# The first keys, values and queries of the cross attention computed in the slot attention's last rounds

## The reference

```python
# slot attention (L0_attn), 16 heads of 128, 64 slots
q, k = rope(hs @ Wq.T), rope(hs @ Wk.T);  v = hs @ Wv.T;  g = hs @ Wg.T
s  = clip(hs @ Ws1.T @ Ws2.T + bs2, -32, 32)
es, enz = exp(s), exp(-cumlogsumexp(s))
A  = tril(q @ k.T * scale)
qv = softmax(enz * (A @ es))
W2 = tril((qv * enz) @ es.T);  o = W2 @ v
out = (rms(o) * g_norm * silu(g)) @ Wo.T
# cross attention (L0_xattn), 16 heads of 16, 257 image and 1344 text keys
q = rms_norm(x @ q_w.T + q_b, norm_q_w)
k, v         = rms_norm(txt @ k_w.T + k_b, norm_k_w),         txt @ v_w.T + v_b
k_img, v_img = rms_norm(img @ k_img_w.T + k_img_b, norm_k_img_w), img @ v_img_w.T + v_img_b
out = (attention(q, k_img, v_img) + attention(q, k, v)) @ o_w.T + o_b
```

## Time and profile before

| | |
|---|---|
| median of 3 runs | 2198.05 us (2189.47 to 2202.49) |
| profiled execution | 2200.9 us |
| its span, first to last instruction | 2199.2 us |
| mean granted TensorE clock | 0.908 |
| busy PE, DVE, ACT, POOL | 1807.4, 1362.2, 839.0, 467.6 us |
| slot attention, from the trace | 0 to 685.6 us |
| cross attention, first load to first exponential's scores | 685.66 to 828.85 us |

### The profile page before, as it was taken

One profiled execution on the slowest core, in us unless ns is written; L12 is line 12 of the kernel. 1 busy time (PEld: TensorE's weight loads), 2 busy tenths in 40 slices (PEclk: granted clock), 3 DMA queues, 4 the chain that ended last, 5 costly groups with the idle time before them and its releaser, 6 DMA issues.

```text
span 2199.2 us, 32217 instructions
## 1 busy us (share of the span) xinstructions
PE 1807.4 (82%) x12150; PEld 1121.8 (51%) x12150; DVE 1362.2 (62%) x3113; ACT 839.0 (38%) x1339; POOL 467.6 (21%) x694
## 2 busy tenths in 40 slices
PE   5789888888864738898998997998597598899977
PEld 4678778777753203343443444565254244444446
DVE  4665666666643645868777844343546587888844
ACT  2233333333321203554645561343122145566652
POOL 4243433433211200201001003143100011311110
PEclk8899999999986758999999997999798789899989
DMA  3010000000004391441726307263722116556100
GB/s 125 1 30 10 20 20 11 10 1 1 1 1 104 125 146 34 91 61 41 127 43 108 44 2 273 96 235 117 130 59 41 51 27 113 92 89 74 28 1 20
DMA packets 88996, 142.96 MB, mean 65 GB/s; under 512 B 14421, under 2 KB 56537, under 8 KB 88842
## 3 DMA queue, kind: packets, MB, share of 16 engines
q1 hardware_dynamic: 74658, 116.05, 25.8%
q10 hardware_dynamic: 12312, 19.71, 3.2%
q0 software_dynamic: 1872, 5.13, 0.6%
HBM read 108.28 MB, written 32.03 MB: 64 GB/s over the span
## 4 chain that ended last, share of the span: by engine, by line
PE 57%; DVE 19%; issue 7%; DMA 6%; ACT 6%; POOL 2%; SPq 2%; ACTq 1%; another core or an unknown queue 0%; POOLq 0%; DVEq 0%
PE bank L1101 8%; PE bank L1061 8%; PE bank L1080 6%; PE bank L1416 5%; PE bank L1751 5%; PE bank L651 3%; PE bank L1647 3%; PE bank L1770 2%; PE bank L1648 2%; PE bank L1649 2%; DVE xa_part_max L1174 2%; PE bank L2160 2%; DMA xa_qst<-xa_negT 1%; PE bank L2145 1%; PE bank L616 1%
## 5 line engine op out<-in xcount | busy, mean ns | idle before, releaser
L1174 DVE TENSOR_REDUCE xa_part_max<-bank 128x1 f32<-128x448 f32 (+1 forms) x512 | 273.7, 569 | 87.2 <-PE bank L1061 82.4
L1135 ACT ACTIVATE xa_e<-bank 128x1024 f32<-128x1024 f32 (+1 forms) x208 | 212.6, 1022 | 146.6 <-PE bank L1080 144.8
L1135 ACT ACTIVATE ca_e<-bank 128x1024 f32<-128x1024 f32 (+2 forms) x208 | 196.4, 956 | 99.7 <-PE bank L1080 90.8
L1174 DVE TENSOR_REDUCE ca_part_max<-bank 128x1 f32<-128x400 f32 (+1 forms) x384 | 205.8, 570 | 35.5 <-PE bank L1061 31.6
L1061 PE MATMUL bank<-xa_kst,xa_qst 122*128 122x448 bf16 (+1 forms) x512 | 172.8, 364 | 45.5 <-issue 25.3
L1061 PE MATMUL bank<-ca_kst,ca_qst 125*128 125x400 bf16 (+2 forms) x512 | 160.3, 349 | 24.9 <-DMA ca_qst<-ca_q_parts 11.9
L1080 PE MATMUL bank<-xa_qst,xa_kst 128*128 128x256 bf16 (+1 forms) x832 | 130.1, 280 | 23.7 <-DMA xa_qst<-xa_negT 23.7
L1101 PE MATMUL bank<-xa_e,xa_vaug 128*17 128x256 f32 (+2 forms) x1792 | 142.3, 393 | 1.6 <-ACT xa_e L1135 0.6
L853 POOL TENSOR_TENSOR gsa_qk<-gsa_qk,gsa_rot 128x512 f32<-128x512 f32 x64 | 81.8, 1278 | 260.6 <-DVE gsa_rot L771 260.6
L1101 PE MATMUL bank<-ca_e,ca_vaug 128*17 128x256 f32 (+2 forms) x1664 | 125.8, 375 | 9.3 <-ACT ca_e L1135 8.4
L1061 PEld LDWEIGHTS bank<-xa_kst,xa_qst 122*128 122x128 bf16 x512 | 48.7, 99 | 155.0 <-DVE xa_part_max L1174 80.4
(11 more groups left out here) (366 smaller groups left out, 4000.7 us busy)
## 6 DMA issues: line engine op xcount, KB each, us to landing
xa_kst<-xa_k_parts SPq DMA_DIRECT2D x96, 200.1 KB, 8.7
ca_kst<-ca_k_parts SPq DMA_DIRECT2D x96, 200.1 KB, 7.4
xa_k_parts<-xa_parts SPq DMA_DIRECT2D x8, 1200.8 KB, 6.5
ca_k_parts<-moe_ctx_parts SPq DMA_DIRECT2D x8, 1200.8 KB
moe_gu<-in_expert_gate_up SPq DMA_DIRECT2D x8, 1024.0 KB
shared<-in_ctxT_split ACTq DMA_DIRECT2D x4, 1601.0 KB, 6.8
moe_ctxT<-in_ctxT SPq DMA_DIRECT2D x8, 800.5 KB, 8.1
ca_cv<-in_ctx ACTq DMA_DIRECT2D x4, 1536.0 KB
```

Of the source, the lines that this page charges most:

```text
L1135: e.activation(self.e[m % 3][0:rows, :, first:T], banks[m % 2][0:rows].rearrange("p a (h t) -> p (a h) t", t=T)[:, :, first:T], ACT.Exp, s ...
L1174: e.tensor_reduce(top, work[:, 0:hi - lo], AX.X, ALU.max).then_inc(*reduced(t, *step))
```

## The change

1. Buffers. `shared` (the context) is allocated outside both stages, so it may be filled during the slot attention. The slot attention's raw weights share two buffers instead of four (q with v, k with g), `clip` is gone (clipping writes into `es`, and the wait for its readers moves from ScalarE to VectorE), and tensors are laid out so that what the cross attention needs first lies on buffers whose last reader is early. The queries get a buffer of their own, two tiles and three parts large.
2. Steps. `xa_early` adds: context fetch and weights in round 12, biases and clearing of `xa_vaug0` in round 14, keys and values of batch 0 (13 `kv` tiles) in round 16, queries of batch 0 and the turning of the keys in round 17, queries of batches 1 and 2 in round 18. The queries of batch 3 are spread over the first units of the cross attention. `behind` starts after 8 steps of a round instead of 4.
3. PSUM rings by the engine that empties them: banks 0 and 1 VectorE, bank 2 `ok` alone, 3 to 5 ScalarE, 6 and 7 both. All moved steps work on banks 0 and 1.
4. The stage of the cross attention starts with the loads of the stacks; weights for its output and the copies into `places_h` follow. The constant rows are bf16 in the table and go from DRAM straight into the stacks. In the differential attention they are loaded at the stage's start into a buffer of their own; VectorE casts nothing.

```diff
-        w_raw = {key: sb(f"w{key}", [P, DC, GK]) for key in LINEAR}
+        raws = [sb(f"w{i}", [P, DC, GK]) for i in range(2)]
+        w_raw = {key: raws[key in "kg"] for key in LINEAR}
...
+            def xa_early(m):
+
+                if m == GSA_UNITS - 4:
+                    yield "fetch", 0
+                    yield "xa_w", 0
+                if m == GSA_UNITS - 2:
+                    yield "xa_w", 1
+                    yield "xa_const", 0
+                if m == GSA_UNITS:
+                    yield "xa_w", 2
+                    for n in range(XA_TILES):
+                        yield "kv", 0, n
+                    yield "fetch", 1
+                if m == GSA_UNITS + 1:
+                    yield from queries(0)
+                    yield "k_norm", 0
+                    yield from xa_keys(0)
+                if m == GSA_UNITS + 2:
+                    yield from queries(1)
+                    yield from queries(2)
...
-                yield from weave(list(weave(list(scores(m)), list(ahead(m)))), list(behind(m)), lead=4)
+                main = list(weave(list(weave(list(scores(m)), list(ahead(m)))), list(behind(m)), lead=8))
+                yield from weave(main, list(xa_early(m)))
...
-        gsa_front, gsa_back = Ring(3), Ring(3)
+        on_dve, on_act, on_both, xa_r1 = Ring(2), Ring(3), Ring(2), Ring(2)
         gsa_order = placed(gsa_steps(), {
+            "es": [(on_dve, clipped)], "cs": [(on_dve, enz_ready)], "qk": [(on_dve, rotated)],
+            "u": [(on_act, u_ready)], "et": [(on_act, et_ready)], "v": [(on_act, v_ready)], "a": [(on_act, a_copied)],
+            "z": [(on_act, z_ready)], "w2": [(on_act, w2_copied)], "ot": [(on_act, ot_ready)],
+            "gate": [(on_both, g_ready)], "o": [(on_both, o_ready)], "wo": [(on_both, x_ready)],
+            "norm_turn": [(on_both, hT_ready)],
...
-                    if k == 0 and unit >= 2:
-                        q.wait_ge(ok_taken, unit - 2)
+                    if k == 0 and unit:
+                        q.wait_ge(ok_taken, unit - 1)
...
-            parts = [list(XA.flow()), [(-100, ("fetch", 0))], spread(queries(), -100, -80)]
-            for b in range(B):
+            parts = [list(XA.flow()), spread(queries(B - 1), 4, 10)]
+            for b in range(1, B):
...
         def xa_sp(q):
             e = q.e
+            for n in range(AHEAD):
+                XA.load_sp(q, n)
+            e.dma_start(xwo[:], a["xa_o_w"].rearrange("(c p) n -> p c n", p=P)).then_inc(*xo_in("xa", by=16))
+            e.dma_start(bo[:], a["xa_o_b"].partition_broadcast(P)).then_inc(*xo_in("xa", by=16))
             e.dma_start(wgate[:], a["gate_w"].rearrange("(c p) n -> p c n", p=P)).then_inc(*gate_in("moe", by=16))
             e.dma_start(h_dram[:, D:D + 2], a["unsent"]).then_inc(*places_filled("moe", by=16))
...
         def da_act(q):
             e = q.e
+            ca_stacks.constants_load(q, ca_aug[:])
...
-                elif kind == "ahead" and n == 0:
-                    ca_stacks.constants_dve(q, cv[:].rearrange("p n d -> p (n d)")[:, 0:CTX])
```

More of the change, by code:

```diff
@@ L94, in const_table @@
     put("sin", np.concatenate([np.sin(ang), -np.sin(ang)], 0).astype(np.float32))
[L96 to L100, removed]
+    aug = np.zeros((P, CTX + CTX % 2), np.uint16)
+    one = np.uint16(0x3F80)
+    aug[REST - 6:REST - 3, :TXT] = one
+    aug[REST - 3:REST, TXT:CTX] = one
+    aug[2 * REST - 3:2 * REST] = one
+    put("aug", aug.view(np.float32))
     key = np.arange(CTX)
@@ L194, in placed @@
 def placed(steps, rings, *tag):
-    return [(step, [ring.take(signal, *(() if step[0] == "norm_turn" else tag), *step) for ring, signal in rings.get(step[0], ())])
+    return [(step, [ring.take(signal, *(own or (() if step[0] == "norm_turn" else tag)), *step) for ring, signal, *own in rings.get(step[0], ())])
             for step in steps]
@@ L537, in gsa_pe @@
                 if kind == "norm_turn":
-                    norm_pe(q, step, places, bank[5:8])
+                    norm_pe(q, step, places, bank[6:8])
+                    continue
+                if kind in XA_EARLY:
+                    xa_pe_step(q, step, places, bank[0:2])
                     continue
@@ L541, in gsa_pe @@
                     (j, free), = places
-                    ps = bank[5 + j] if kind in ("z", "w2", "gate", "o", "ot", "wo") else bank[j]
+                    ps = home(kind, j)
                     if free:
@@ L694, in gsa_act @@
                     q.wait_ge(v_mm, n, i)
-                    e.copy(v[n % 2][:, i, :], bank[j]).then_inc(*v_ready(*step))
+                    e.copy(v[n % 2][:, i, :], home(kind, j)).then_inc(*v_ready(*step))
                 elif kind == "a":
@@ L705, in gsa_act @@
                 elif kind == "z":
-                    ps, zb = bank[5 + j], qz[n % 2]
+                    ps, zb = home(kind, j), qz[n % 2]
                     if n < 2:
@@ new lines, in __init__, with constants_load, constants_act @@
+                row = 0 if sets == 2 else REST
+                self.aug = a["consts"][row:row + REST, lo:hi].bitcast(BF16)[:, 0:keys]
+            def constants_load(self, q, to):
+                q.e.dma_start(to, self.aug).then_inc(*self.aug_in(self.tag, by=16))
+            def constants_act(self, q, staged=None):
+                aug = self.aug if staged is None else staged
+                if staged is not None:
+                    q.wait_ge(self.aug_in, self.tag)
+                for t in self.kst:
+                    q.e.dma_start(t[self.rows], aug.unsqueeze(1).broadcast_to([REST, UNIT, self.keys])).then_inc(*self.aug_copied(self.tag, by=16))
@@ L1385, in build, with xa_pe_step @@
             "out_turn": [(xa_work, out_copied)], "out": [(xa_work, x_ready)], "norm_turn": [(xa_work, hT_ready)]}, "xa")
+        def xa_pe_step(q, step, places, work):
+            e = q.e
+            kind, n, *rest = step
+            if not places:
+                return
+            j, free = places[0]
+            ps = work[j]
+            if free:
+                q.wait_ge(*free)
+            if kind == "q":
+                q.wait_ge(hT_ready, "norm_turn", 1, n)
+                q.wait_ge(xq_in, "xa")
+                for c in range(DC):
+                    m = e.matmul(ps[:, 0:D], hT[:, c, n * P:(n + 1) * P], xwq[:, c, :], start=(c == 0), stop=(c == DC - 1))
+                m.then_inc(*q_mm(n))
+            elif kind == "q_turn":
+                q.wait_ge(q_scaled, n)
+                for c in range(DC):
+                    m = e.transpose(ps[:, c * P:(c + 1) * P], qq[:, n % TB, c * P:(c + 1) * P], ident[:])
+                m.then_inc(*kt_mm(*step))
+            elif kind == "kv":
+                m_, = rest
+                k0 = xa_tiles[m_][0]
+                q.wait_ge(xc_in, "xa", n)
+                q.wait_ge(xw_in, "xa")
+                for (r0, r1, s, _, _) in xa_tiles[m_][2]:
+                    for c in range(DC):
+                        m = e.matmul(ps[r0:r1, :], xctx[:, c, k0 + r0:k0 + r1], wkv[s][:, c, :], start=(c == 0), stop=(c == DC - 1))
+                m.then_inc(*kv_mm(n, m_))
+            elif kind == "k_turn":
+                m_, = rest
+                rows = xa_tiles[m_][1]
+                q.wait_ge(k_scaled, n, m_)
+                for c in range(DC):
+                    m = e.transpose(ps[:, c * P:c * P + rows], kk[0:rows, m_, c * P:(c + 1) * P], ident[0:rows, 0:rows])
+                m.then_inc(*kt_mm(*step))
```

554 lines of the change are left out of this document (278 added, 276 removed).

## The result

The changed kernel takes 2112.72 us (median; 2109.28 to 2121.28) against 2200.27 for the kernel before on the same chip: ratio 0.9614, 95% interval 0.9566 to 0.9661. In a later group of runs the changed kernel was measured again, at 2122.13 against 2198.88: ratio 0.9638 (0.9601 to 0.9674). Ratios leave out slow executions: there was one, of the kernel before (5748 us), beside the first four experiments.

What follows compares the result with a forecast made beforehand. Bounds named: TensorE's waits in the slot attention, the emptiest stretch before the cross attention's first exponential, and VectorE's constants load. -65 + 40 - 15 + 3 - 8 = -45 gave 2156, as median 2153 us; range 2120 to 2192.

Steps and rivals of the forecast that it cites:

- Part 3: Slot attention: PSUM rings by emptying engine remove bank waits of projections and `a`; gain 15 us, bounds 0 and 31.
- the rings give all they can: Rival, slot attention: the new PSUM rings gain 31 us instead of 15, total 2137 us; chance 6%.
- Part 2: Slot attention rounds 16 to 18: the moved cross attention work costs 40 us, bounds +6 and +62.
- Part 1: Cross attention start: the transfer queue sets the first exponential at 78 us instead of 143.2; gain 65 us.
- Part 4: Last batch's queries in the cross attention cost 3 us; differential attention's constants, loaded early without a cast, gain 8.
- The rounds hide nothing: Rival, last slot attention rounds: streams hold each other, moved work costs its upper 62 us, total 2175; chance 20%.
- The queue isn't the limit: Rival, cross attention start: `negT` arrives soon after issue, first exponential at 45 us, total 2120; chance 13%.
- Slower, through the single `ok` bank: Rival, slot attention: a unit's first `ok` waits for VectorE's `sm_max`; at 4.5 us each 2220 us; chance 7%.

Runs made afterwards that it cites:

- the early fill: Changed kernel with the small rows of `in_unsent` and three copies of x into `moe_places_h` issued in slot attention round 12: 2107.29 us, ratio 0.9587.
- the fourth bank with the weave: Kernel before with a fourth bank in its shared front ring, one `ok` bank, trailing work from the ninth step: 2153.97 us, ratio 0.9799.
- the two behind it: Changed kernel with first `negT` ahead of half the loads and constant rows held back, 2090.92 us; the same with trailing work from the thirteenth step, 2104.27 us.

## Why the prediction was wrong

Its direction and its mechanism for most of the gain were right; the sum was 43 us short. By its steps:

**The step that failed is Part 3** ("I take half, gain 15 us", upper bound 31). By unit 14 the slot attention is 41.9 us ahead. Three errors are in it. The weave's `lead` stands in the diff and had no price at all; on top of the rings it is worth 11.7 us at this mark (40.1 against 28.4) and 7.6 at the end of the stage. The bank waits were halved on the ground that TensorE would run sooner into a data wait; it did (`qz` 10.5 to 18.7 us, and `ogT` came up), yet rings alone gave 28.4. And the bound of 31 counted idle time only: a third of what the rings gave in eight rounds was busy time of the same products, which had run at the lower level of the clock behind the waits. The rival "the rings give all they can" (31 us) was the right one for the rings, and even it was below the whole. The reason of Part 3, that v and `a` no longer share banks with what VectorE empties, was not needed for the gain: one more shared bank does the same.

**Part 2, the moved work in the last rounds, was right.** From unit 14 to the stage's end the kernel with rings and weave takes 85.0 us and the changed kernel 123.9: 38.9 us, 40 forecast. The same pair without the weave gives 40.9 (80.9 and 121.8), and against the kernel before, with 80.2, it is 43.7. Of these 43.7 us, 21.0 come before the softmax product of unit 15 (635.8 and 614.8) and 22.7 after it, where the forecast had 20 for round 16 and 18 for the two behind. TensorE's busy time there grows from 51.6 to 83.1 us, so 31.5 us of its work cost 38.9. Its largest waits from 545 us to the end of the stage are those of the queries' own chain and of the norm:

```profile
PE bank L1460 <- DVE xa_qq L1560: 18.5, 3, 8.8
PE bank L344 <- DVE h L333: 7.8, 3, 4.7
```

The stage ended at 687.6 and not at 711 because of Part 3.

**Part 1 was right in kind and 11 us short.** 66.6 us instead of 78, with the engines full from the start to 752.3. The term that was mis-sized is the backlog, 64.9 us instead of 75.5: the constants (9 us) and weights (1.5) cost nothing that can be seen. Without the fill, loads, constants and weights take as long as the loads did alone. DMA of the kernel with the early fill, 682 to 730 us (packets, MB, share of 16 engines), beside the 5.72 MB in 46 us of the earlier trace rows:

```profile
q1 hardware_dynamic: 5039, 6.34, 85.3%
q10 hardware_dynamic: 576, 1.64, 17.0%
```

8.0 MB in 46 us is 173 GB/s, where the loads alone went at 124. The fill then is 65 less 46, 19 us, as priced (14.2 + 4.8). The Trainium skill (DMA: Bandwidth & Descriptors, "Issuing engines are not separate DMA queues") says that DMAs of all issuing engines run on the same 16 DMA engines and interleave. The forecast read this as times that add, and in this trace they do not: with the constants the sum was 78, without them 69, and 66.6 was measured. What the Trainium skill says in the section "Queues, rings and completion order" of that page, that each DMA engine takes a ring's descriptors in order, is borne out as far as it goes: 8.8 us behind a full queue, 4.9 in an empty one. What I missed here is that SP itself was held, 16.2 us, in issuing copies that nobody needed yet. Some 8.3 of these are what the same issues take in a nearly idle queue (round 12 of the run with the early fill, DMA share 0.07 before them).

**Part 4.** The constants of the differential attention: 7.6 us between the marks before and at its first maximum (81.0 to 88.6), 8 forecast. The last batch's queries: forecast +3, measured -1.5 from first to last exponential (487.8 to 486.3). Two more executions, of the changed kernel (494.7) and with the weave undone (488.8), show that this stretch scatters by more than that; the term is neither shown nor refuted.

**Not forecast: 4.8 us between the cross attention's end and the experts** (76.2 to 81.0). Before has a stop there in which VectorE and ScalarE stand until an unnamed releaser:

```profile
ACT moe_tg L1797 <- remote: 7.2, 1, 7.2
DVE x L1926 <- remote: 2.1, 1, 2.1
```

It is in all eight profiles of the first two groups of experiments, with the change and without it, and in none of the four of the last group (the fourth bank with the weave, the changed kernel again and the two behind it), nor in the changed kernel's first. So it goes with the group of runs and with none of the edits, and I leave its cause open.

Together against the profiled executions: 26.9 more from Part 3, 11.5 from Part 1, 4.5 from the last queries, 4.8 from the stop, 3.7 less from Part 2 as the marks have it (123.9 against 80.2 from unit 14 to the end, 43.7) and 0.2 less elsewhere are 43.8 over the forecast's 45: the 88.8 between the spans. In the second measurement of the changed kernel the gain is 77, so some 10 of these 43 us may be the measurement's and not the change's.

**Rivals.** "The rounds hide nothing" is out, Part 2 being at 38.9. "The queue isn't the limit" is out: with `negT` issued at 39 us it still landed at 48 behind loads. "Slower, through the single `ok` bank" is out: no wait of `ok` for its bank is in any profile.

## What to carry to other kernels

Price every edited number, the weave's `lead` too, before halving a bound: what had no term in the forecast was worth 8 to 10 us at the end of the stage with the new rings, and 24 with the old ones. When TensorE waits for a bank, first ask whether a bank can be had from somewhere: here one more shared bank gave all that the grouped rings gave with it; grouping without it was not run. And put small transfers that a chain waits for ahead of bulk ones on the same queue, and bulk ones that depend on nothing where the queues are empty.

## What was not expected of the hardware

- A full DMA share isn't a rate: 16 engines at 99.6% moved 124 GB/s with one queue of key and query rows, and full engines 173 GB/s with a second queue's constants and the weights among them. Which of these made the difference no run shows.
- A short wait of TensorE can cost more than its length: behind waits of 2.0 to 3.1 us the lower level of the clock was granted, five times in 300 us, and once with the rings. With 15.9 us of waits gone, the same 1663 products also took 7.7 us less.
- Issuing is not free, and less so when a queue is full: three copies of x held SP for 8.3 us in a nearly idle queue and for 16.2 us in a full one, and the six small DMAs behind them took 7.8 us to issue instead of 3.8.
